# Four chained cross-attention layers: keys and values in one stage on four banks, and a 16-head layer with rounded maxima, grouped value products and one load of x

## The reference, cut to what matters

```python
q = hidden_states @ Wq ; k = encoder @ Wk ; v = encoder @ Wv      # 1024 wide
logits = q.k^T * 64 ** -0.5
col_bias[:, token_indices_A] = (-20 * (1 - mask_A))[:, None]
col_bias[:, token_indices_B] = (-20 * (1 - mask_B))[:, None]
out = softmax(logits + col_bias) @ v ; out = out @ Wo + bo + residual
```

```python
q = rmsnorm(x) @ wq ; k = cond @ wk ; v = cond @ wv
out = x + softmax(q.k^T / sqrt(32)) @ v @ wo
```

## Time and profile before

| | us |
|---|---|
| median of 3 runs | 4637.84 (4637.76 to 4638.88) |
| the profiled execution, its own time | 4637.64 |
| its span, first to last instruction | 4635.9 |
| TensorE busy | 4336.0 (94%) |
| VectorE busy | 2565.3 (55%) |
| ScalarE busy | 1986.6 (43%) |
| GpSimd busy | 1809.3 (39%) |
| mean granted TensorE clock | 0.976 of 2.4 GHz |

### The profile page before, as it was taken

The page is one execution under the profiler, slowest core; times in us unless marked ns, Lnnn a source line. Parts: engine busy times, 40 slices in busy tenths (PEclk is TensorE's granted clock), DMA queues, the critical chain, the costliest instruction groups (busy, mean ns, idle before and its releaser), DMA issues. The chain is left out here.

```text
span 4635.9 us, 63591 instructions
## 1 busy us (share of the span) xinstructions
PE 4336.0 (94%) x20066; PEld 2694.6 (58%) x20066; DVE 2565.3 (55%) x3575; ACT 1986.6 (43%) x2444; POOL 1809.3 (39%) x923
## 2 busy tenths in 40 slices
PE   7999799996999999999978999999999998999998
PEld 6888588883556555655644554544554554455454
DVE  2122200014555455545447777787777777777776
ACT  2111211112333333333325566566656656666665
POOL 0000000002353444344434556555555555555655
PEclk9999899997999999999988999999999999999999
DMA  4333422224444444444442223322322322232233
GB/s 155 130 127 131 155 80 82 79 88 131 107 115 115 109 102 120 115 109 113 107 125 62 81 73 90 88 83 81 92 81 75 94 84 86 82 88 79 77 95 97
DMA packets 301729, 461.95 MB, mean 100 GB/s; under 512 B 44955, under 2 KB 95131, under 8 KB 301693
## 3 DMA queue, kind: packets, MB, share of 16 engines
q1 hardware_dynamic: 301692, 461.50, 34.4%
HBM read 227.88 MB, written 102.76 MB: 71 GB/s over the span
## 5 line engine op out<-in xcount | busy, mean ns | idle before, releaser
L813 DVE TENSOR_REDUCE a_max_cols<-a_ps 128x1 f32<-128x512 f32 x2072 | 1323.4, 677 | 329.4 <-PE a_ps L937 327.0
L707 ACT ACTIVATE a_probs<-a_ps 128x1024 f32<-128x1024 f32 x1024 | 1018.6, 1027 | 735.8 <-PE a_ps L958 732.7
L937 PE MATMUL a_ps<-a_k_ops,a_q_ops 96*128 96x512 f32 (+1 forms) x2592 | 955.0, 433 | 42.7 <-DVE a_max_cols L813 30.9
L937 PEld LDWEIGHTS a_ps<-a_k_ops,a_q_ops 96*128 96x128 f32 (+1 forms) x2592 | 459.8, 190 | 627.0 <-DVE a_max_cols L813 490.9
L958 PE MATMUL a_ps<-a_q_ops,a_k_ops 128*128 128x512 f32 x2560 | 780.0, 407 | 36.3 <-ACT a_probs L707 20.7
L595 POOL TENSOR_TENSOR a_probs<-a_probs 128x1024 f32<-128x1024 f32 x192 | 463.3, 2413 | 726.9 <-PE a_ps L974 705.7
L974 PE MATMUL a_ps<-a_probs,a_v 128*32 128x512 f32 (+1 forms) x4096 | 674.6, 610 | 0.0
L958 PEld LDWEIGHTS a_ps<-a_q_ops,a_k_ops 128*128 128x128 f32 x2560 | 462.5, 190 | 215.7 <-ACT a_probs L707 104.4
L595 POOL TENSOR_TENSOR a_sums<-a_probs 128x1024 f32<-128x1024 f32 x192 | 454.3, 2385 | 5.0 <-ACT a_probs L707 5.0
L595 POOL TENSOR_TENSOR a_sums<-a_sums,a_probs 128x1024 f32<-128x1024 f32 x192 | 455.2, 2390 | 0.3
L601 POOL TENSOR_TENSOR a_qn_lo<-a_qf,a_qn_hi 128x512 fp32r<-128x512 f32 x99 | 126.7, 1280 | 791.2 <-ACT a_qn_hi L662 791.2
(11 more groups left out here) (92 smaller groups left out, 5615.5 us busy)
## 6 DMA issues: line engine op xcount, KB each, us to landing
a_k_ops<-k_scratch SPq DMA_DIRECT2D x201, 256.0 KB, 4.0
a_q_ops<-a_qn_hi SPq DMA_DIRECT2D x792, 64.0 KB, 2.0
k_scratch<-kp_out SPq DMA_DIRECT2D x88, 512.0 KB, 2.8
a_q_ops<-a_qn_hi SPq DMA_DIRECT2D x268, 128.0 KB, 2.3
a_x_raw<-out_t SPq DMA_DIRECT2D x26, 1024.0 KB, 5.3
a_q_ops<-a_qn_lo SPq DMA_DIRECT2D x396, 64.0 KB, 2.0
a_x_res<-out_t SPq DMA_DIRECT2D x96, 256.0 KB, 3.1
out_t<-a_results SPq DMA_DIRECT2D x96, 256.0 KB, 2.0
```

The lines of the kernel that those rows point to most:

```text
L707: act.activation(probs[:, s], ps[:, 2 * (s % 2):2 * (s % 2) + 2, :], ACT.Exp)\
L813: dve.tensor_reduce(max_cols[:, col:col + 1], bank(MAXB[n]), AX.X, ALU.max, negate=True).then_inc(reduced, 1)
L937: last = pe.matmul(bank(MAXB[n]), q_ops[0:rows(p), s, h, p, q * P:(q + 1) * P], k_ops[0:rows(p), s, k_head(h), p, :], start=(p == 0), stop ...
```

## The change

`project_contexts` takes the place of both calls of `project_context`. It has four PSUM banks, three buffers for raw pieces, and weights that come as column blocks (128 columns of all 1024 rows) behind the work: the first key block needs one column block and a quarter of the context. The value weights overwrite the key weights column by column during the last key batch, all through the one buffer `LAST_RAW`. During the last two batches of values, x and the query weights of layer 0 are loaded and split into tiles that `a0` shares, and the bias rows are made, as 128 x 4 tiles, and stored to DRAM. In `a0` the operands are laid out so that hi·hi and the bias stand in one pass, `maxima` takes that pass alone (one matmul in place of two) on banks 4, 7 and 5, `outputs` stand together behind the last of them, the denominators go to bank 3 and are copied to SBUF by ACT before DVE takes the reciprocals, POOL's sums have a tensor of their own, x is loaded whole in tile 0, the first three queries are projected to three banks, and the output weights are rounded behind the three queries. `a1` gets the shared tiles; its loop keeps its instructions.

```diff
+def project_contexts(nc, ctx_t, wk, wv, k_scratch, v_scratch, first, bias, bias_rows):
+    RAW = 3
+    START = [("c", 0), ("w", 0), *(("c", j) for j in range(1, NCH)), *(("w", n) for n in range(1, 5))]
+    EARLY = 5
+    LAST_RAW = RAW - 1
+    BANKS = 4
...
+        def weights_behind(bb, par, n, last):
+            if isinstance(bb, int) and bb == 0 and par == 0 and 0 <= n < KB - EARLY:
+                return EARLY + n
+            return KB + n if last and par == 1 and n >= 0 else None
...
+            def keys(bb, last):
+                        sp.wait_ge(k_taken, b * KB + n + 1)
+                        sp.dma_start(k_scratch[b, n].rearrange("c p s -> p c s"), as_f32(out[m % 2][:, :, :]))\
+                            .then_inc(k_stored[m % 2], DMA)
+                        if n in CHUNK_AT:
+                            load_c_behind(0 if last and par == 1 else b + 1, b + 1, CHUNK_AT[n])
+                        w = weights_behind(bb, par, n, last)
+                        if w is not None:
+                            sp.wait_ge(w_split, w)
+                            load_w(w)
...
+                        behind(k_taken, b * KB + n, 2 if m < 2 else BANKS)
+                            if n == 0 and k % 2 == 0:
+                                pe.wait_ge(c_split, b * NCH + k // 2 + 1)
+                            if k == 0:
+                                pe.wait_ge(w_split, n + 1)
...
+                        if n < VP:
+                            pe.wait_ge(w_split, KB + (c0 + w) // P)
...
-    XAT = (M - 1,) if has_norm else (3, M - 1)
-    OUT_AT = (2, 3, 5, NS - 1) if has_norm else (1, 2, 3)
+    XAT = (M - 1,) if has_norm else (1, 4)
+    OUT_AT = (2, 3, 5, NS - 1) if has_norm else ()
-        x_raw = sb("x_raw", [P, XT, S], F32)
-        x_res = sb("x_res", [P, RS, S], F32) if has_norm else x_raw[:, 1:2, :]
+        x_raw = sb("x_raw", [P, CK, S], F32)
+        x_res = sb("x_res", [P, RS, S], F32)
-        sums = sb("sums", [P, H // 2, 2, S], F32) if has_norm else probs[:, 0:H // 2]
+        sums = sb("sums", [P, H // 2, 2, S], F32)
-        OUTB, DENB = 6, (3 if has_norm else 7)
+        OUTB, DENB = 6, 3
-        MAXB = 5 * (4, 7, 5) + (4,) if has_norm else (4, 5, 4, 5, 7, 4, 5, 4)
+        MAXB = (6 * (4, 7, 5))[0:M]
+        def q_bank(t, early):
+            return bank((QB, TURNB, OUTB)[t] if early else QB)
-                    for i, part in enumerate((qn_hi, qn_hi, qn_lo)):
+                    for i, part in enumerate((qn_lo, qn_hi, qn_hi)):
...
+            if not has_norm:
+                for c in range(HALF):
+                    round_chunk(HALF + c, c, 1)
+                act.wait_ge(w_split, HALF)
...
-                        if t == SPLIT_AT and s in ((3,) if has_norm else (1, 3)):
+                        if t == SPLIT_AT and s in ((3,) if has_norm else (0, 2)):
-                    if has_norm:
-                        take_denominators(it, t)
                     shift(*place(it, t + 1))
                     if not has_norm:
+                        take_denominators(it, t)
                         round_q(*place(it, t + AHEAD))
...
-                        if t > 0 and n == 0:
-                            if not has_norm:
-                                reciprocals(it, t - 1, range(PARTS - 1, PARTS))
-                            else:
-                                normalise(it, t - 1)
-                        if t > 0 and n == 1 and not has_norm:
+                        if t > 0 and n < 2 and not has_norm:
+                            reciprocals(it, t - 1, range(EARLY + n, EARLY + n + 1))
+                        if t > 0 and n == (0 if has_norm else 2):
                             normalise(it, t - 1)
...
-                for p in range(PASS):
-                    last = pe.matmul(bank(MAXB[n]), q_ops[0:rows(p), s, h, p, q * P:(q + 1) * P],
-                                     k_ops[0:rows(p), s, k_head(h), p, :], start=(p == 0), stop=(p == PASS - 1))
-                last.then_inc(smax, 1)
+                pe.matmul(bank(MAXB[n]), q_ops[0:SHIFT, s, h, PASS - 1, q * P:(q + 1) * P],
+                          k_ops[0:SHIFT, s, k_head(h), PASS - 1, :], start=True, stop=True).then_inc(smax, 1)
...
-                    if not has_norm:
-                        outputs(it, t, KT - 1)
+                    if has_norm:
+                        denominators(it, t)
                     else:
-                        denominators(it, t)
+                        for kt in range(KT):
+                            outputs(it, t, kt)
                     turn(*place(it, t + 1))
```

587 lines of the change are left out of this document (343 added, 244 removed).

## The result

The changed kernel takes 4513.51 us (median of 4 runs, 4511.72 to 4515.04) against 4638.11 for the kernel before: a ratio of 0.9731, 95% interval 0.9714 to 0.9748. That is 125 us less. The forecast was 4475, so 38 us of the expected 163 did not come; the measured time lies in the range, and the direction is the forecast one. One of the six executions of the last experiment, e9, took 11211.01 us where the other five took 4419.8 to 4423.41; nothing on record explains it, and without it the median of e9 would be 4422.96 in place of 4423.13.

A forecast was written before the change was run, and what follows sets the result against it. It saw three slow starts costing some 120 us and 16-head tiles set closely by VectorE's chain and TensorE. Terms -19 - 6 - 22 - 27 - 89 = -163 from 4637.6 gave 4475 us, range 4430 to 4525.

The forecast's parts named there:

- Start of the keys: First key blocks: needing one weight column block and a quarter of the context starts matmuls earlier, -19 us.
- four banks: Key and value blocks: fewer TensorE waits for evictions and restarts, -6 us (bounds -3 and -9).
- keys to values: Passage from keys to values: weights arrive behind the work, but one raw buffer leaves a 12 us wait; -22 us.
- 1.7 more at a lowered clock: Start of values: extra TensorE time after the 12 us wait for weights, counted within the -22 us.
- Into the 16-head layer: Last value matmul to first scores: 42.3 us in place of 69.6, -27 us (bounds -33 and -15).
- each of the next two queries costs a spread round of 6.9: Entry to the 16-head layer: second and third query each take 6.9 us, the last out at entry + 25.4.
- The middle tile: 16-head layer: VectorE's serial chain, maximum, value matmuls and turn give 15.9 us against 16.70, -5.6 a batch.
- the rival's tile of 13.6: 16-head layer rival: TensorE, not VectorE, sets the tile at 13.6 us, total 4346; chance 0.06.
- the two splits of x now stand in VectorE's chain, 1.2 each: 16-head layer, once a batch: the splits, the second partly behind the last bank's release, add 1.6 us.
- Value products eating the gain: 16-head layer rival: VectorE's chain plus sixteen value products stays as long as before, total 4518; chance 0.12.
- Slow column loads: Key and value starts, rival: weight column blocks take 6.4 us each to land, total 4506; chance 0.10.
- The falling clock: 16-head layer rival: TensorE's short waits lower its clock, tile 19.5 us, total 4677; chance 0.04.

The follow-up runs named there:

- e9: Changed kernel with x splits after the last maxima, one value group earlier, first query's loads ahead, output weights rounded between queries, two value-weight buffers: 4423.13 us.
- e5: Changed kernel with two buffers in turn for the value weights in place of one: 4501.47 us.
- e10: Changed kernel with two PSUM banks in place of four for keys and values: 4519.62 us.
- e3: Changed kernel with the first query's loads issued ahead of the keys of tiles 1 and 2 and the values: 4508.05 us.
- e4: Changed kernel with the first query's loads ahead, plus output weights rounded and split between the three queries, not behind the third: 4503.48 us.
- e8: Changed kernel with maxima of two matmuls again in place of one: 4533.27 us.
- e6: Changed kernel with one of the four value groups moved forward, behind the sixth maximum: 4468.19 us.
- e7: Changed kernel with three value groups back where they stood before, behind the fourth, sixth and eighth maximum: 4609.56 us.
- e1: Changed kernel with both splits of x behind the seventh and eighth maximum in place of the second and fifth: 4473.12 us.
- e2: Changed kernel with the splits of x behind the fourth and eighth maximum, the first still ahead of the fifth reduction: 4515.97 us.

## Why the prediction came out 38 us short

**Start of the keys, four banks, keys to values.** Right in size and cause: -20.0 for the start (-19 forecast), loads of 4.3 us (4.3 taken), 6.8 us a column block and 10.6 of waiting (6.7 and 12), -48.8 for the whole against -47. e5 shows that the wait was the one buffer, and e10 that four banks are worth 7.0 in this stretch (-6 forecast), though as 11.6 less 4.6 behind it: two of my terms were coupled and I had added them. The "1.7 more at a lowered clock" had no row behind it; the clock is 0.50 from 512.36 to 517.50 and 0.92 up to 523.00, which makes some 3 us. Three side sums of the prediction do not come out. By its own cycle, loads of 3.6 leave a wait of 4 and not 7 (its -30 goes with 4); loads of 6.4 with the 0.3 added make a cycle of 9.1 and a wait of 38, and the 35 goes with a cycle of 8.8; and 7 x 0.8 x 8 is 45, where 43 was added. None of them moves the forecast.

**Into the 16-head layer.** -17.9 for -27. The failed step is "each of the next two queries costs a spread round of 6.9". The round from the second to the third was 6.8. The first took from 1001.4 to 1017.8, with two pieces of output weights, nine loads of keys and one of values issued in the 10 us ahead of it. The row that I took the round from (1083.70 to 1090.61) stood 40 us behind its keys, which SyncE had begun to issue at 1041.91 in the trace of before, and behind one last piece of output weights and one of values issued at 1075.98 and 1076.39, which landed in 5.2 and 5.5 us. So it shows an empty queue: its copies landed 2.3 us behind their issue, where the first query's now took 10.8. e3 shows that what lies ahead matters, and that reordering gives 3.8 of the 9 us back. That the bytes have to pass at some time before the third query is my reading of it; no run takes them away. The 4.4 of e4 are another thing, the rounding behind the third query, which the forecast had counted.

**The middle tile.** Right: 15.98 for 15.9, with VectorE's ring as its cause, link by link. e8 confirms this from one side (more TensorE work hides) and e6 from the other (0.77 of the 0.86 us that leave the place behind the last maximum is gained). What I had wrong is what the parts are worth. TensorE's work fell from 16.53 to 14.85 us a tile, by 1.7 and not by 3.1, so the rival's tile of 13.6 was out of reach. Taken back one at a time, the rounded maxima are worth 20 us, and the grouping 96 (e7), more than the whole gain of the layer, because with the other edits the normalisation ends only after TensorE has come to the place of the first group. The prediction priced the grouping at nothing of its own and named it only as a risk. Its use is that no value product stands in front of scores and maxima with a wait for the normalisation; how many may come forward again is another matter, and e6 shows that one group is better there. ScalarE's copy of the denominators and GpSimd's sums in a tensor of their own were not taken back singly, so what they cost or give stays open.

**The tile with the splits.** Here some 27 of the 38 us are: 3.4 a batch in this tile, and 0.4 a batch each in the middle tiles together and in tile 0. The failed step is "the two splits of x now stand in VectorE's chain, 1.2 each [...]: +1.6". The tile is 5.3 over a middle one, 5.0 on average, not 1.6. First, the split took 2.52 beside GpSimd's sum, and I had kept the 1.88 of rows 8 as the price. I had also misread that row. The sum of 3.25 that I put beside the 1.88 ended 4.2 us before that split began. The partners of the two are missing from rows 8. In the timeline of VectorE and GpSimd of the kernel before, they are the split that met the sum of 3.25, and the sum that met the split of 1.88:

```profile
1679.09 1.21 DVE L819 TENSOR_TENSOR a_x_lo<-a_x_raw,a_x_hi 128x1024 fp32r<-128x1024 f32 x1
...
1685.21 2.35 POOL L595 TENSOR_TENSOR a_probs<-a_probs 128x1024 f32<-128x1024 f32 x1 [0.16 <-POOL a_probs L595]
```

The sum of 3.25 started 0.2 us behind the split of 1.21 and was the one held up; the others of that tile take 2.35 to 2.38. The split of 1.88 started 0.80 us before the sum of 2.35 ended, and ended 1.08 behind it. So in both the later one was held until the earlier one had ended, and the 1.88 was short only because little of the sum was left. The same 1.1 us from the GpSimd instruction's end to the split's end stand in every tile of the changed kernel, e1, e2, e6, e8 and e9 in which a split of 128 x 1024 starts beside one, whether the split then shows 1.53, 2.52, 2.77, 2.80 or 3.28. The Trainium skill (page "SBUF — State Buffer", section "Who interferes with whom") has an exclusive lock. The rows agree with the page: 1.21 in a gap between sums, up to 3.28 beside them, and a sum that starts in a split's time takes 3.14 in place of 2.38. Second, behind a wait of 2.46 on TensorE the clock fell, in all eight batches, and made 3.65 us of matmuls 6.15. I had that mechanism as a rival for *every* tile and priced it at zero for this one, though rows 10 showed it in the very tile that this one replaces: 7.10 us of window with a stall of 2.84, clock 0.79. e1 takes both away with one tuple and gives 4473, what was forecast. That the two numbers agree is partly luck: the entry's missing 9 us stand in e1 against splits that cost 0.2 a batch where the forecast had 1.6, 11 us in all.

**Rivals.** Value products eating the gain: no (15.98), though e6 shows that fewer of them at the ring's end give more. Slow column loads: no (4.3 us a load, 6.8 a column block). TensorE-bound: no (1.1 us idle). The falling clock: 0.97 over the layer, and not in the changed kernel's middle tiles, whose waits are 0.35 and 0.69; but the tile with the splits shows that rival's mechanism, and e7 in middle tiles, with 16.96, 18.55 and 19.80 for the same work. The Trainium skill (page "TensorE: Matmul & The Clock Gate", section "A second HAM failure mode: psum-queue depth-cycling") ties the swing to TensorE's short idling between groups through banks. Here the changed kernel cycles through three banks with waits of under 0.7 us and keeps 1.00, so the runs show the page's swing only behind single waits of 2.03 us and more, and there not each time.

What stays open: what separates the tiles of e7 and e8 that keep the clock from those that lose it, with equal waits; and 0.3 us a batch of what e9 lacks.
